# A graph attention layer with a top-2 expert layer on one core: the seam between attention and experts is dealt anew

## The reference, cut to what matters

```python
# x: (8, 1024, 128) float32; adj: (1024, 1024), about 3% ones; 4 heads of 32
def gnn(h):                       # h = layernorm(x)
    q, k, v = h @ Wq.T + bq, h @ Wk.T + bk, h @ Wv.T + bv
    s = clip(q k / sqrt(32), -10, 10);  s = where(adj == 0, -10, s)
    o = softmax(s) v @ Wo.T + bo + h
    return layernorm(o) * gamma + beta
x = x + gnn(layernorm(x))
def ffn(h):                       # h = layernorm(x), 8 experts, hidden 256
    mask = one_hot(top_k(h @ Wg + bg, 2)).sum()
    return sum over the two chosen experts e of gelu(h @ W1[e] + b1[e]) @ W2[e] + b2[e]
out = x + ffn(layernorm(x))
```

## Time and profile before

| what | us |
|---|---|
| three runs | 746.49, 747.64, 751.01; median 747.64 |
| the profiled execution | 748.67 |
| its span, first to last instruction | 746.9 |
| busy in the span | PE 692.4, DVE 602.4, POOL 581.3, ACT 506.0 |

### The profile page before, as it was taken

One profiled execution on the slowest core, in us unless ns is written; L12 is line 12 of the kernel. 1 busy time (PEld: TensorE's weight loads), 2 busy tenths in 40 slices (PEclk: granted clock), 3 DMA queues, 4 the chain that ended last, 5 costly groups with the idle time before them and its releaser, 6 DMA issues. The chain is left out here.

```text
span 746.9 us, 17044 instructions
## 1 busy us (share of the span) xinstructions
PE 692.4 (93%) x5420; PEld 358.4 (48%) x5420; DVE 602.4 (81%) x1310; ACT 506.0 (68%) x1029; POOL 581.3 (78%) x673
## 2 busy tenths in 40 slices
PE   5798999999999999999999999897788899999994
PEld 2232233333333333333333333332287889999994
DVE  3689989999999999999999998899775765555552
ACT  4655576787777777777777777655586656667662
POOL 7639776988889888898988989887666776667664
PEclk9998999999999999999999999999899999999998
DMA  7540000010110101111011000041313243333330
GB/s 266 179 123 29 0 29 6 25 43 22 44 37 29 44 22 37 43 30 43 16 44 43 15 30 15 29 135 37 91 45 90 80 129 109 93 87 97 103 86 1
DMA packets 47958, 45.42 MB, mean 61 GB/s; under 512 B 6981, under 2 KB 42576, under 8 KB 47872
## 3 DMA queue, kind: packets, MB, share of 16 engines
q1 hardware_dynamic: 41888, 31.60, 15.0%
q0 software_dynamic: 5984, 12.74, 4.9%
HBM read 27.73 MB, written 18.34 MB: 62 GB/s over the span
## 5 line engine op out<-in xcount | busy, mean ns | idle before, releaser
L754 ACT ACTIVATE e<-e 128x2048 f32<-128x2048 f32 x128 | 245.1, 1915 | 155.5 <-DVE e L977 155.5
L977 DVE SCALAR_TENSOR_TENSOR e<-scores_ps,bound_mem 128x2048 f32<-128x2048 f32 x128 | 293.2, 2291 | 35.7 <-PE scores_ps L444 29.8
L852 ACT ACTIVATE e<-scores_ps,bound_mem 128x128 f32<-128x128 f32 x364 | 104.0, 372 | 52.6 <-PE scores_ps L611 52.6
L1449 POOL TENSOR_TENSOR ctx_part<-ctx_part,z_inv 128x1024 f32<-128x1024 f32 x60 | 115.7, 1928 | 27.4 <-DVE z_inv L993 27.4
L463 PE MATMUL z_ps<-e,one_column 128*32 128x512 f32 x1024 | 136.5, 605 | 0.0
L1476 POOL DMA_INDIRECT out<-e,near x91 | 92.0, 1011 | 50.5 <-POOL near L1469 28.5
L1461 POOL TENSOR_TENSOR ctx_sum<-ctx_sum,ctx_part 128x512 f32<-128x512 f32 x90 | 115.3, 1282 | 8.0 <-POOL ctx_sum L1461 0.4
L611 PE MATMUL scores_ps<-e,bound_mem 128*128 128x128 f32 x728 | 97.3, 277 | 2.3 <-DVE bound_mem L1168 1.0
L985 DVE STREAM_TRANSPOSE ctx_part<-ctx_ps 128x512 f32<-128x512 f32 x128 | 90.4, 706 | 1.4 <-PE ctx_ps L456 1.3
L611 PEld LDWEIGHTS scores_ps<-e,bound_mem 128*128 128x128 f32 x728 | 88.5, 192 | 4.5 <-issue 3.4
L1423 POOL DMA_INDIRECT sorted_rows<-x_rows,slot x64 | 63.6, 993 | 25.9 <-issue 17.0
(11 more groups left out here) (181 smaller groups left out, 1015.4 us busy)
## 6 DMA issues: line engine op xcount, KB each, us to landing
near<-sorted_rows SPq DMA_DIRECT2D x91, 130.0 KB, 2.2
near<-in_x SPq DMA_DIRECT2D x16, 256.0 KB, 2.9
bound_mem<-in_adjT SPq DMA_DIRECT2D x4, 1024.0 KB, 10.3
x_post<-in_x SPq DMA_DIRECT2D x16, 256.0 KB, 2.8
sorted_rows<-pad_row SPq DMA_DIRECT2D x1, 3640.0 KB, 15.2
out<-e,near POOLq DMA_INDIRECT x91, 2.3
sorted_rows<-x_rows,slot POOLq DMA_INDIRECT x64, 2.5
bound_mem<-in_w SPq DMA_DIRECT2D x1, 1024.0 KB, 6.1
```

Source lines behind the costliest of these rows:

```text
L754: nc.scalar.activation(every, every, ACT.Exp, scale=SCORE_SCALE).then_inc(exp_done, 1)
L852: nc.scalar.activation(e_flat[:, h_at:h_at + P], scores_ps[:, i % 2, k * P:(k + 1) * P], ACT.Gelu, bias=part_flat[:, bias_at:bias_at + 1]) ...
L977: dve.scalar_tensor_tensor(out=e[:, s % E_RING], in0=scores_ps[:], scalar=-CLIP, in1=to, op0=ALU.max, op1=ALU.min).then_inc(clipped, 1)
L1449: nc.gpsimd.tensor_tensor(pair, pair, z_inv[:, v % 2, j:j + 2].to_broadcast([P, 2, SQUARES, DH]), ALU.mult).then_inc(ctx_scaled, 1)
```

## The change

Attention keeps the steady order to the end of block 15: the last two blocks lose their own order. There are two tables: tiles 0 to 20 after block 11, tiles 21 to 90 after block 15. Block 12's scatter goes behind attention, and what is left of blocks 12 to 15 is dealt out over the slots anew. The small columns of the tables are no longer copied out of PSUM, and several of the table's operations now write to PSUM (`table_row`, `table_col`). `XT_RING` goes from 9 to 16, `O_RING` from 6 to 14, and ACT copies the weights of 6 tiles in place of 12. POOL's stores are no longer tied to their slots: `stored_by(k)` lets them trail by six until slot 24; from slot 25 on every second slot stores one tile more, until slot 35, and from there slot k again stores tile k-2; a tile's mask now comes directly before its own store. The diff, cut:

```diff
-XT_RING, XN_RING, W_RING, H_RING, O_RING = 9, 3, 3, 3, 6
-COPIED_ACT = 12
+XT_RING, XN_RING, W_RING, H_RING, O_RING = 16, 3, 3, 3, 14
+COPIED_ACT = 6
...
-GROUPS = [(12, 0, sure(12)), (14, sure(12), sure(14)), (15, sure(14), FFN_TILES)]
+GROUPS = [(11, 0, sure(11)), (15, sure(11), FFN_TILES)]
 REST = len(GROUPS) - 1
+GROUP_END = {v: g for g, (v, _, _) in enumerate(GROUPS)}
 GROUP_OF = {at: g for g, (_, at, _) in enumerate(GROUPS)}
 MASKED_AT = GROUPS[REST][1]
 LONGEST = max(end - at for _, at, end in GROUPS)
+EDGES = max(LONGEST, TOKENS // P)
 SLOTS = FFN_TILES + 2
...
+def stored_by(k):
+
+    return FFN_TILES if k >= SLOTS - 1 else max(0, min(k - 1, k - 7 + max(0, (k - 25) // 2 + 1)))
...
-twice_ps = table_ps[REST][:, 2 * P:2 * P + GROUPS[REST][2] - GROUPS[REST][1]]
+TABLE_AT = 2 * P + 16
+table_ps = [job_ps[0][:, TABLE_AT:BLOCK], job_ps[1][:]]
+N_AT, TILES_AT, END_AT, BEGIN_AT, LEFT_AT, OFFSETS_AT, LOOKUP_AT = 0, 1, 2, 3, 4, 8, 16
...
     sp.dma_start(wide[:, :, HIDDEN:WAY_IN], b1T.rearrange("p (e k) -> p e k", k=2))\
         .then_inc(experts_loaded, 16)

+    load_post(LAST)
     sp.wait_ge(spare_padded, 16 * 2)
     sp.wait_ge(q_filled, BLOCKS)
     for i in range(FFN_TILES):
             sp.wait_ge(table_ready, g + 1)
             for k in range(3):
                 sp.wait_ge(scattered[k], 16 * TILES * len(range(k, GROUPS[g][0] + 1, 3)))
-        if i == XT_RING:
-            load_post(BLOCKS - 1)
         at = sp.value_load(table[0:1, i, 0:1], min_val=0, max_val=SPARE * P)
         r = i % XT_RING
...
+    def offset_columns():
+        pe.wait_ge(q_ready, BLOCKS)
+        pe.wait_ge(gate_drained, 12)
+        for k in range(3):
+            ins = pe.matmul(table_col(0, OFFSETS_AT + k), offsets_row[:, k, :], one_row[:, 0:1],
+                            start=True, stop=True)
+        ins.then_inc(offsets_filled, 1)
...
                 values(2)
             if j == 7:
                 queries(2)
-        last = u == BLOCKS - 1
-        if j == 0 and not last and is_block(u - 3):
+        last = u == LAST
+        if j == 0 and is_block(u - 3):
             turn_xn2(u - 3)
-        if j == (0 if last else 1) and is_block(u - 3):
+        if last and j == 0:
+            columns(0)
+        if j == 1 and is_block(u - 3):
             gate(u - 3)
         if j in (1, 2) and is_block(u - 2):
             values(u + 2)
         if j == 7 and u > 0 and is_block(u + 2):
             queries(u + 2)
-        if j == (1 if last else 5) and is_block(u - 3):
+        if j == 5 and is_block(u - 3):
             rank(u - 3)
+        if u == LATE and j == 3:
+            offset_columns()
         if last and j == 3:
-            columns(0)
-        if last and j == 4:
             ends(0)
-        if last and j == 5:
+        if last and j == 7:
             lookup(0)
-        if j == 7 and u >= LATE:
-            turn_xn2(u - 2)
-
+
+context(STEPS - 2)
+context(STEPS - 1)
+turn_xn2(13)
 for k in range(SLOTS):
     if k < FFN_TILES:
         turn_tile(k)
-    if k < LAG:
-        context(STEPS - LAG + k)
     if k == 0:
+        project(14)
         gate(13)
-    if k == 11:
-        turn_xn2(14)
-    if k == 12:
-        project(15)
-    if k == 13:
-        rank(14)
-    if k == 16:
-        columns(1)
     if k == 18:
         ends(1)
-    if k == 20:
-        turn_xn2(15)
-    if k == 21:
-        lookup(1)
-    if k == 23:
-        rank(15)
-    if k == 24:
-        columns(2)
-    if k == 26:
-        ends(2)
-    if k == 29:
-        lookup(2)
     if k >= 2:
         load_ways_out(k - 2)
     if 1 <= k <= FFN_TILES:
         first_product(k - 1)
-    if k == 2:
+    if k == 3:
         rank(13)
-    if k == 11:
-        gate(14)
-    if k == 21:
-        gate(15)
+    if k == 7:
+        turn_xn2(14)
+    if k == 8:
+        project(15)
+    if k == 10:
+        rank(14)
+    if k == 14:
+        turn_xn2(15)
     if k >= 2:
         second_product(k - 2)
-    if k == 2:
-        project(14)
+    if k == 8:
+        gate(14)
+    if k == 14:
+        gate(15)
+    if k == 15:
+        rank(15)
+    if k == 16:
+        columns(1)
+    if k == 18:
+        lookup(1)
...
             drain_k(u + 2)
         if j == 6 and u > 0 and is_block(u + 2):
             drain_v(u + 2)
-        if j == (7 if u < LATE else 6) and is_block(u - 2):
+        if j == 7 and is_block(u - 2):
             normalise_x2(u - 2)
         if j == 7 and u > 0 and is_block(u + 2):
             drain_q(u + 2)
-        if j == 7 and u >= LATE:
-            drain_xn2T(u - 2)
-
+
+drain_xn2T(13)
+act.wait_ge(z_added, STEPS)
 for k in range(SLOTS):
-    if k == 0:
-        act.wait_ge(z_added, STEPS - 1)
-    if k == E_RING - 1:
-        act.wait_ge(z_added, STEPS)
+    if k == 1:
+        square_proj(14)
+    if k == 7:
+        drain_xn2T(14)
     if k < FFN_TILES:
         drain_turned(k)
     if k < COPIED_ACT:
         load_ways_in(k)
         copy_weights(k)
-    if k == 4:
-        square_proj(14)
-    if k == 5:
+    if k == 2:
         normalise_proj(14)
+    if k == 6:
+        normalise_x2(14)
+    if k == 8:
+        square_proj(15)
     if k == 9:
-        normalise_x2(14)
-    if k == 11:
-        drain_xn2T(14)
+        normalise_proj(15)
     if k == 13:
-        square_proj(15)
-    if k == 15:
-        normalise_proj(15)
-    if k == 19:
         normalise_x2(15)
-    if k == 21:
+    if k == 14:
         drain_xn2T(15)
     if 1 <= k <= FFN_TILES:
...
+        if v in GROUP_END:
+            dve.tensor_tensor(n_row[:, GROUP_END[v], :], ranks[0:1, TILES, :], first_rank[0:1, 0, :], ALU.subtract)\
+                .then_inc(n_row_ready, 1)
...
     def find_owners(g):
         one, n = slice(g, g + 1), GROUPS[g][2] - GROUPS[g][1]
         dve.wait_ge(end_filled, g + 1)
-        dve.tensor_copy(end_col[:, one], table_ps[g][0:NP, 8:9]).then_inc(end_ready, 1)
-        dve.wait_ge(end_ready, g + 1)
-        dve.tensor_tensor(begin_col[:, one], end_col[:, one], t_col[:, one], ALU.subtract)\
+        dve.tensor_tensor(table_col(g, BEGIN_AT), table_col(g, END_AT), t_col[:, one], ALU.subtract)\
             .then_inc(begin_ready, 1)
-        dve.tensor_scalar(inside[:, g, 0:n], count_f[:, 0:n], end_col[:, one], None, ALU.is_lt)\
-            .then_inc(inside_ready, 1)
+        dve.tensor_tensor(past[:, g, 0:n], table_col(g, END_AT).to_broadcast([NP, n]), count_f[:, 0:n], ALU.is_gt)\
+            .then_inc(past_ready, 1)
         dve.wait_ge(begin_ready, g + 1)
-        dve.wait_ge(inside_ready, g + 1)
-        dve.scalar_tensor_tensor(out=owner[:, g, 0:n], in0=count_f[:, 0:n], scalar=begin_col[:, one],
-                                 in1=inside[:, g, 0:n], op0=ALU.is_ge, op1=ALU.mult)
-        dve.tensor_scalar(from_col[:, one], done_col[:, one], begin_col[:, one], float(P), ALU.subtract, ALU.mult)\
+        dve.tensor_tensor(table_row(g, 0), table_col(g, BEGIN_AT).to_broadcast([NP, n]), count_f[:, 0:n], ALU.is_le)\
+            .then_inc(begun_ready, 1)
...
+        dve.tensor_tensor(owner[:, g, 0:n], table_row(g, 0), past[:, g, 0:n], ALU.mult).then_inc(owner_ready, 1)
...
         if u == 3 and j == 2:
             dve.wait_ge(rows_loaded, 16 * 5)
             dve.wait_ge(consts_ready, 1)
-        if u < LATE and is_block(u - 3):
+        if is_block(u - 3):
             if j == 2:
                 find_best(u - 3)
             if j == 3:
                 find_places(u - 3)
             if j == 4:
                 mark_pair(u - 3)
-        if u >= LATE and j == (3 if u == LATE else 0):
-            choose(u - 3)
         if j == 4 and is_block(u + 3):
             begin_statistics_x(u + 3, range(1 if u else 0, TILES))
         if j == 5 and is_block(u - 2):
             begin_statistics_x2(u - 2)
-            if u >= LATE:
-                end_statistics(ln["3"], u - 2)
         if j == 6 and is_block(u + 3):
             end_statistics(ln["1"], u + 3)
-        if j == 6 and u < LATE and is_block(u - 2):
+        if j == 6 and is_block(u - 2):
             end_statistics(ln["3"], u - 2)
-        if j == (7 if u < LATE else 6 if u == LATE else 2) and is_block(u - 3):
+        if j == 7 and is_block(u - 3):
             place(u - 3)
         if u == 1 and j < EXPERTS - 1:
             sum_biases(j)
-        if u == BLOCKS - 1:
-            if j == 2:
-                count_rows(0)
-            if j == 3:
+        if u == LATE and j == 4:
+            keep_offsets()
+        if u == LAST:
+            if j == 0:
                 count_tiles(0)
             if j == 4:
                 find_owners(0)
+            if j == 6:
                 find_rows(0)
-            if j == 5:
+            if j == 7:
                 write_table(0)

+turn(STEPS - 2)
+turn(STEPS - 1)
+turn_sum(14)
+invert_sums(15)
 load_offsets(0)
 for k in range(SLOTS):
+    if k == 1:
+        scale_last(4)
+        choose(13)
+        add_last(1)
+    if k == 3:
+        scale_last(6)
+    if k == 4:
+        statistics_x2(14)
+    if k == 6:
+        add_last(5)
```

(165 more changed lines are left out.)

139 lines of the change are left out of this document (58 added, 81 removed).

## The result

The kernel after takes 758.5 us (median of 4 runs, 757.9 to 761.9) against 747.1 (4 runs, 746.2 to 751.0) on the same chip: ratio 1.0143, 95% interval 1.0104 to 1.0182. It is slower, by 1.4%. The forecast of 735.7 and its range of 727 to 748 are both missed; the third rival (POOL becomes the bound, 758.2) is what happened.

A forecast was written before the change was run, and what follows sets the result against it. PE alone bounds tiles 28 to 90 (1.896 us a tile), unchanged; gains lie before. 748.67 - 8.8 (attention's end) - 3.6 (front) + 0.5 (last stores) = 736.8 profiled, 1.03 above the median: 735.7, range 727 to 748.

The forecast's parts named there:

- the third rival: POOL's stores: mask-to-store gap 0.80, 2.14 us a store against PE's 1.896, last store 22.5 late, 758.2 us; chance 0.07.
- the part on POOL's stores: From tile 21: mask-to-store gap 0.30, a store every 1.64 us, lag of 5.7 gone within 22 tiles; +0.5 at the end.
- C: The end of attention's last clip, the zero point for forecast times in the expert stage.
- The point of decision: POOL's stores from tile 21: the POOL rival decides from 1.81 us a store on.
- Attention's end: Blocks 14 and 15: 30.5 us, and 31.2 with the last clip; a gain of 8.8, bounds 5.5 and 11.
- The start and tiles 0 to 27: Expert stage's front: first product 8.3 us after the last clip, tile 28's 77 instead of 80.6; gain 3.6.
- Block 14's chain: Beside tiles 0 to 7: scaling, residual, statistics, two stores, root, done 21.3 us after the last clip; ACT waits about 1.
- DVE as the bound of tiles 8 to 20: DVE needs 1.61 us a tile, 20.9 for thirteen, plus 11.6 of other work; PE itself would need 31.
- The give-back rival: Front of the expert stage stalls, tile 28's first product 85 us after the last clip, 743.7 us; chance 0.20.
- the one at PE's pace: DVE's extra work falls into idle time, tile 28's first product 69.1 us after the last clip, 727.8 us; chance 0.13.
- The copies and POOL: Six tiles' weight copies moved to DVE add nothing to POOL; the skill's rule would hold POOL up to 2.9 us more.
- the sum: Whole kernel: 748.67 - 8.8 - 3.6 + 0.5 = 736.8 for the profiled execution, forecast 735.7 as median; chance 0.60.

The follow-up runs named there:

- a1: Kernel after with POOL masking tile i+1, not tile i, just before storing tile i: 733.2 us, ratio 0.9813 to the kernel before.
- c3: Kernel after with a masked store's two waits swapped, mask's wait first, then the result's: 756.1 us, ratio 1.0105 to the kernel before.
- b2: Kernel before with two intermediate rows of the first expert table (inside, row_in) in PSUM instead of SBUF: 747.5 us, ratio 0.9984.
- a5: Kernel after with masks made by DVE and the tables' intermediates in SBUF instead of PSUM: 733.5 us, ratio 0.9814 to the kernel before.
- c1: Kernel after with each mask one store ahead and ACT copying twelve tiles' weights instead of six: 733.8 us, ratio 0.9804 to the kernel before.

## Why the prediction was wrong, point by point

**The step that failed** is in the part on POOL's stores: "I take 1.64, because the store's wait for the result is long over and its preparation can run beside the mask". The gap from a mask to its own store was put at 0.30; it measured 0.85, a store every 2.08, and 2.14 on the mean, where I took 1.64. The store's start was not prepared beside its own mask; with the mask of another tile in the same place (a1) the gap was 0.16. The row nearest to the new situation was the other bound, 0.80 from DVE's result to the store that waits for it: there too a producer has just ended. I took the 0.30, which is the gap of a store whose conditions had been met for long. The 0.55 of the earlier trace rows misled as well. It counts from the other tile's mask; the result that this store waited for is this row of DVE's timeline before, which ends at 650.77, 0.80 ahead of the store:

```profile
650.48 0.29 DVE L1186 TENSOR_TENSOR e<-ctx_ps,bound_mem 128x128 f32<-128x128 f32 x1 [0.40 <-PE ctx_ps L637]
```

a1 has the same 0.55 at 720.22, at PE's pace.

**The rival's numbers held.** It said 2.14 a store, 22.5 us late, 758.2. Measured: 2.14, 22.45 us at tile 90, 758.5. That the time came out within 0.3 us is luck in part, because its errors cancel. Store 21 started 8.2 us behind its result and not 5.7, since block 15's scatters were out at C + 55.3 and not C + 53. The 14 result buffers hold a lag of 21.4 us, after which PE waits and the lag grows no more: from tile 72 on PE lost 3.8 us, which the rival did not have. And the 735.7 from which it counted was 2.5 above what the schedule gives without the late stores (733.2, a1). One of PE's waits:

```profile
692.71 1.13 PE L622 MATMUL scores_ps<-e,bound_mem 128*128 128x128 f32 x8 [0.29 <-ACT e L857]
```

The chance of 0.07 was too low: the rows of before had the 0.80 for every store that waited. The point of decision, 1.81 us a store, was not tested closely: 1.42 (a1) catches up, 2.08 (c3) and 2.14 (after) do not.

**Attention's end: 8.8 forecast, 10.4 measured.** Block 14 took 30.37 (30.5 forecast), block 15 with its last clip 29.71 (31.2): the table's operations cost less than the 2.1 allowed and took their places beside PE. The clock stayed at 1.00. DVE's rows, against the earlier trace rows:

```profile
513.47 0.17 DVE L1119 TENSOR_TENSOR owner<-job_ps,past 28x21 f32<-28x21 f32 x1
...
520.96 0.23 DVE L1140 SCALAR_TENSOR_TENSOR row_of<-job_ps,home,owner 28x21 f32<-28x21 f32 x1
521.12 2.27 DVE L978 SCALAR_TENSOR_TENSOR e<-scores_ps,bound_mem 128x2048 f32<-128x2048 f32 x1
```

The cause that I gave, waits for POOL, is shown by b2; but b2 and a5 also show that it was not these waits alone that made block 15 long in time that counts: without them the old schedule won nothing, with one of them back the new one lost 0.9. My reading of the rest, argued and not tried alone, is the steady order: block 13's statistics on DVE start 22.7 us into block 15 where they started 29.3 us into it. One piece of it stands in the rows: in the kernel before and in b2 POOL issues two scatters of block 12 between block 13's residual and its root, and from that residual (L1437 after, L1445 in b2) to the root's first operation pass 10.1 us in b2 and 7.8 after, where these scatters have gone behind attention.

**The start and tiles 0 to 27: right in the sum.** First product at C + 8.5 (8.3), tile 28's at C + 77.1 (C + 77). Block 14's chain was added up wrongly: C + 14 and 2.7, 1.6, 2.6 and 1.9 make C + 22.8, not C + 21.3, and POOL's shift was there at C + 23.1. So ACT waited for it 2.16 us where I had said 1, and the Gelu of tile 5 ended at C + 25.8, not C + 24.1. At tile 28 nothing of this is seen; that DVE's own list covered it is my reading, not tried. The spacing from tile 28 was 1.896 until the ring was full. DVE as the bound of tiles 8 to 20 is supported by c1. The give-back rival (tile 28 at C + 85) and the one at PE's pace (C + 69) both fell. The reason given for the table's operations, that rows 2 show copies and sums with a PSUM side, points at rows that are not there; b2 has them.

**The copies and POOL: right.** I added nothing for the six tiles' copies that moved to DVE. The trace agrees: 70 stores of the kernel after take 1007 ns on the mean, 69 of a1 997, and the last one of a1, with no copy left, 0.98 us. The rule of the Trainium skill ("SBUF — State Buffer", section "A bandwidth-pool intuition that's wrong (but worth ruling out)") that a DVE copy in a two-port mode holds back a POOL-issued DMA's descriptors is not seen at this size here. What decided was POOL's wait for its own mask.

**With the one step mended** the sum stood: a1 is the change with stores as cheap as the forecast wanted them, 735.7 forecast, 733.2 measured, in place of 758.5. It is faster than both kernels, by 1.9% than the one before (interval 1.3% to 2.5%).

## What to carry to other kernels

When an instruction is moved next to the DMA that needs it, price the DMA by a row of the same DMA in which its producer has just ended, not by one in which all was ready; here that is 0.8 us against 0.16, on an engine with 1.9 us a tile. A producer of 0.2 us belongs one item ahead of its consumer, even on the same engine. And a wait whose cause is understood is still worth nothing until the trace says what stands next behind it.

## What the runs showed that was not expected

A store on POOL starts, but for a few, 0.79 to 0.86 us after the last of its waits is met, be it POOL's own 0.2 us operation directly ahead or DVE's result, and in either order of the two waits; if all were met before, it starts 0.16 us after a POOL operation and 0.30 after another DMA. The last two are odd side by side: a mask between two stores costs less than its own length, 1.38 us with it against 1.29 without.

This does not hold for every indirect DMA of POOL. A scatter of the same kernel starts 0.27 us after the result of DVE that it waits for (kernel after, DVE's row and POOL's; 0.29 in the kernel before, where POOL had been idle for 8.6 us):

```profile
573.42 0.25 DVE L1067 TENSOR_REDUCE slot<-own_rank 128x4 uint32<-128x112 f32 x1
...
573.94 0.97 POOL L1424 DMA_INDIRECT sorted_rows<-x_rows,slot  x1 [0.60 <-DVE slot L1067]
```

The two differ in the program: a store has a bounds check (`bounds_check`), and each of the 91 stores has a register move of 29 ns in POOL's queue ahead of it, which the scatters have not. Whether that is where the other half microsecond comes from was not tried. So the 0.80 is known for this store alone.

Some small DVE operations with all operands in SBUF run until the POOL operation beside them ends. In b2 done_col is one: it starts at 519.09 and takes 1.27, and POOL's timeline there has

```profile
519.08 1.27 POOL L1442 TENSOR_TENSOR n<-n,rows 128x512 f32<-128x512 f32 x1
```

In the kernel before there were four such operations; with an input or the output in PSUM owner, row_in and row_of took 0.23, 0.29 and 0.23. fit_col, still all in SBUF, took 0.15 there, with no long POOL operation beside it. It is no rule for all of them: row_of in a5 took 0.23 beside POOL's 1.01, and left_col in the kernel before took 0.13 at the start of POOL's scaling of 1.91:

```profile
521.97 0.13 DVE L1132 TENSOR_SCALAR left_col<-begin_col 28x1 f32<-28x1 f32 x1
```

What tells the two kinds apart the runs don't show.
